# Layer 0's front in another order, values made there, and the maxima's transfers on one queue

## The chip, the core and the metric

One core of a Trainium2 chip runs the whole program in one launch. The metric is the device time of an execution in microseconds; lower is better. TensorE, VectorE (DVE), ScalarE (ACT), GpSimd (POOL) and SyncE (SP) each work through a queue of their own in order, and tell each other by semaphores.

## What is computed

Two layers on x of 32 batches of 256 tokens with 128 channels. Layer 0 is a latent attention with 16 heads, then a top-1 mixture of 8 experts; layer 1 is a windowed attention with pooled latents, then a top-8 mixture of 64 experts. What the change touches is layer 0:

```
xn     = layernorm(x)
latent = xn @ latent_w + latent_b            # 36 columns: keys and values
q      = xn @ Wd_w[h] + Wd_b[h]              # per head
attn   = softmax(causal(q @ latent.T / sqrt(8)))
y      = attn @ latent
x      = x + concat_heads(y) @ out_w + out_b
logits = xn @ Wr + br                        # 8 experts, from the same normalised tokens
```

## The kernel before

Tokens stand in 64 tiles of 128, in eight chunks of eight tiles (XCH, XT). Two heads form a pair (eight pairs), two pairs a group (four groups).

The **front** makes, chunk by chunk: statistics on VectorE (stats0, lines 930 to 938), mean and deviation on GpSimd (deviation0, 617 to 627), normalised rows on ScalarE (norm, 1482 to 1486), transposes on TensorE into two PSUM banks (chunk, 1781 to 1788), their evacuation by ScalarE (chunk, 1488 to 1490) and VectorE (turned, 940 to 942), and the routing logits of the chunk, eight columns for each tile (logits, 1790 to 1798). Beside them run, for the first batch, keys and values (kv, 1800 to 1808), queries (qproj, 1810 to 1820, evacuated by qevac, 1492 to 1497), their casts to bf16 on GpSimd (round_keys and round_queries, 642 to 651), and the row maxima: a score product of a pair (smax, 1822 to 1834), reduced on VectorE (red, 954 to 963) and turned (turn_maxima, 965 to 970). The order of each engine's work in the front is written out by hand (TensorE 1949 to 1984, ScalarE 1530 to 1553, VectorE 1102 to 1132, GpSimd 687 to 704).

The transfers of x are all issued by SyncE: the first chunk at once (331), the other three pieces behind the small weights (342 to 344).

The **steps** follow, one for each batch b, while the maxima of the next batch n are made; a loop holds steps 2 to 29. TensorE's order in a step (1896 to 1947) mixes scores of n (smax), queries of n, the output projection of b-2 (outp), scores of b (st_first, st_second), and the product with the values (av_first, av_second) of four groups. All groups of av share one bank, bankB, which ScalarE evacuates after each (yevac, 1513 to 1515); av_first of the next group waits for that. Between the third and the fourth group stands kv of the batch after the next:

```
                av_first(b, 2, True)
                av_second(b, 2)
                if m:
                    kv(m)
                av_first(b, 3, True)
                av_second(b, 3)
```

VectorE evacuates keys and values in its own kv (944 to 952); for the values it waits until the step before has done its products.

The row maxima enter the scores as two extra rows of the queries: four transfers of 4 KB from mT into qT, two issued by SyncE as soon as mT is there (maxima, 354 to 358), two by ScalarE at the end of its step, behind the last evacuation (maxima, 1499 to 1503, called at 1528). st_first of a batch waits for all four (1839). SyncE's queue then holds, in each step, the denominators of the batch (360 to 388). In the 16 steps of batches 2 to 17 GpSimd also scatters the normalised rows to the sorted order of the experts (scatter_rows, 637 to 640), between round_keys and round_queries.

## Time and profile before

| | us |
|---|---|
| runs, median of 3 (lowest to highest) | 1732.88 (1728.96 to 1735.12) |
| the profiled execution | 1733.61 |
| its span | 1731.9 |
| busy TensorE, VectorE, ScalarE, GpSimd | 1502.6, 1156.0, 992.2, 922.6 |

The profile is of one execution; its time lies 0.7 us above the median. The span is cut into stretches by what TensorE does: the front up to about 97 us, the steps of layer 0's attention to about 796, then the experts of layer 0, layer 1 and its experts, which the change does not touch. In the profile's rows a matmul of fp32 data is two records, one for each of its two passes; PE is TensorE's matmuls, PEld its weight loads; a row "x8" merges eight neighbours of one kind, and what stands in brackets is the idle time of the engine before it and who ended it. SPq and ACTq are transfers issued by SyncE and ScalarE.

### The profile page before, as it was taken

The page shows a single profiled execution, that of the slowest core. Times are in us where ns is not written, and L with a number is a line of the kernel's source. Part 1 is how long each engine was busy: PE and PEld are TensorE (multiplying, and loading weights), DVE is VectorE, ACT ScalarE, POOL GpSimd, SP SyncE. Part 2 cuts the span into 40 slices and gives each one's busy share as a digit, 9 for nine tenths or more (in the row PEclk, how much of TensorE's full clock was granted, in tenths as well). Part 3 has the DMA queues.
Part 4 walks back from the last instruction along what each step waited for, and adds up shares of the span by engine and source line. Part 5 has one row for each costly group of instructions (what it writes and reads, how often), then busy time and mean ns, then how long its engine had stood idle before and what let it go on. Part 6 is the DMA issues. An engine that isn't in the chain of part 4 may idle for free.

```text
span 1731.9 us, 44291 instructions
## 1 busy us (share of the span) xinstructions
PE 1502.6 (87%) x12962; PEld 1083.1 (63%) x12963; DVE 1156.0 (67%) x4123; ACT 992.2 (57%) x2494; POOL 922.6 (53%) x1627
## 2 busy tenths in 40 slices
PE   4789999999999999998996788888888888875883
PEld 4644555555555555556996577777777777764772
DVE  3356656666666666654553599988999989876661
ACT  3334555555555555553331788887888888852431
POOL 4235566666654444434444566666666666623663
PEclk9998999999999999999998699999999999996665
DMA  7103222222222222234332122112112121116444
GB/s 199 36 7 79 63 62 62 62 62 62 62 56 56 62 62 62 69 77 99 68 71 48 28 45 43 44 43 46 42 41 44 44 46 42 42 28 130 88 84 117
DMA packets 240984, 107.60 MB, mean 62 GB/s; under 512 B 145561, under 2 KB 229338, under 8 KB 240858
## 3 DMA queue, kind: packets, MB, share of 16 engines
q1 hardware_dynamic: 228506, 92.97, 22.4%
q0 software_dynamic: 10240, 13.64, 3.7%
q8 instruction: 26, 0.43, 0.1%
q10 hardware_dynamic: 2176, 0.26, 0.1%
q14 instruction: 36, 0.29, 0.1%
HBM read 61.92 MB, written 40.16 MB: 59 GB/s over the span
## 4 chain that ended last, share of the span: by engine, by line
PE 59%; ACT 17%; issue 6%; POOL 6%; DVE 5%; DMA 5%; SPq 1%; POOLq 0%; ACTq 0%; DVEq 0%
PE bankT L1843 8%; PE bankB L1866 8%; PE bankA L1818 7%; PE bankT L2018 4%; PE bankB L1873 3%; PE bankT L1852 3%; ACT pe L1592 3%; DMA qT<-mT 3%; ACT qx L1606 3%; ACT km L1615 2%; PE bankB L1882 2%; ACT gqx L1606 2%; PE bankB L2081 2%; PE bankS L2007 2%; PE bankT L2007 2%
## 5 line engine op out<-in xcount | busy, mean ns | idle before, releaser
L958 DVE CUSTOM_DVE_ANT_0 masked<-bankS,causal 128x128 bf16<-128x128 f32 x512 | 128.6, 289 | 224.0 <-PE bankS L1833 220.0
L658 POOL TENSOR_SCALAR_AFFINE_SELECT probs<-probs 128x512 f32<-128x512 f32 x256 | 171.4, 693 | 146.3 <-ACT probs L1507 146.0
L1507 ACT ACTIVATE probs<-bankT 128x1024 f32<-128x1024 f32 x128 | 131.2, 1025 | 123.5 <-PE bankT L1843 123.5
L961 DVE CUSTOM_DVE_ANT_0 masked<-bankS,causal 128x256 bf16<-128x256 f32 x512 | 195.7, 420 | 0.1
L651 POOL CAST qb<-qT 128x256 bf16<-128x256 f32 x256 | 100.3, 414 | 170.1 <-ACT qT L1496 169.9
L1496 ACT ACTIVATE qT<-bankA,bd 128x256 f32<-128x256 f32 x256 | 107.3, 470 | 117.7 <-PE bankA L1818 113.6
L1818 PE MATMUL bankA<-xnT,wd 128*128 128x256 f32 x512 | 153.5, 425 | 0.0
L1843 PE MATMUL bankT<-qT,kT 37*128 37x512 f32 x512 | 147.1, 651 | 6.5 <-DMA qT<-mT 5.8
L1866 PE MATMUL bankB<-probs,vaug 128*64 128x512 f32 x512 | 139.9, 625 | 1.6 <-ACT yT L1515 1.4
L1309 DVE STREAM_TRANSPOSE pt<-pe 128x768 f32<-128x768 f32 x128 | 124.4, 972 | 24.2 <-ACT pe L1592 24.2
L1515 ACT COPY yT<-bankB 128x512 f32<-128x512 f32 x128 | 74.9, 585 | 113.0 <-PE bankB L1873 113.0
L2137 PE MATMUL bankT<-vx,pt 128*64 128x68 f32 x1024 | 72.4, 228 | 54.1 <-ACT gkm L1635 54.1
L1818 PEld LDWEIGHTS bankA<-xnT,wd 128*128 128x128 f32 x512 | 91.6, 199 | 34.2 <-issue 26.3
L1592 ACT ACTIVATE pe<-pr 128x768 f32<-128x768 f32 x128 | 108.0, 844 | 7.3 <-DVE pr L1303 5.0
L2137 PEld LDWEIGHTS bankT<-vx,pt 128*64 128x64 f32 x1024 | 55.6, 137 | 66.8 <-ACT gkm L1635 34.7
L724 POOL COPY probs<-shelf 128x516 f32 x72 | 44.8, 623 | 77.3 <-DVE qT L1195 74.4
L762 POOL DMA_INDIRECT yg<-ys_sorted,idx_g x64 | 65.9, 1029 | 36.8 <-POOL gate_g L758 26.4
L1873 PEld LDWEIGHTS bankB<-probs,vaug 128*64 128x64 f32 x512 | 37.2, 138 | 74.4 <-issue 73.5
L2018 PE MATMUL bankT<-shelf,qT 128*128 x576 | 78.8, 280 | 0.1
L1831 PEld LDWEIGHTS bankS<-kb,qb 36*128 36x128 bf16 x512 | 26.2, 94 | 83.5 <-issue 66.6
L1852 PE MATMUL bankT<-qT,kT 37*128 37x256 f32 x512 | 78.2, 382 | 0.0
L1873 PE MATMUL bankB<-probs,vaug 128*64 128x256 f32 x512 | 77.9, 383 | 0.0
(306 smaller groups left out, 4231.5 us busy)
## 6 DMA issues: line engine op xcount, KB each, us to landing
rzb<-reciprocals SPq DMA_DIRECT2D x128, 128.0 KB
yT<-yT SPq DMA_DIRECT2D x64, 128.0 KB
xtab<-tab SPq DMA_DIRECT2D x32, 192.0 KB, 2.0
xs_sorted<-zeros SPq DMA_DIRECT2D x1, 4608.0 KB, 18.5
qT<-xs_sorted SPq DMA_DIRECT2D x144, 32.0 KB, 1.7
ys_sorted<-qT SPq DMA_DIRECT2D x36, 128.0 KB, 1.9
value_rows<-vrow SPq DMA_DIRECT2D x32, 128.0 KB, 1.8
vx<-value_rows SPq DMA_DIRECT2D x256, 16.0 KB, 1.8
```

The costliest lines, as they stand in the source:

```text
L658: pool.affine_select(out=blocks, in_=blocks, compare_op=ALU.is_ge, fill=0.0, base=0, pattern=[[0, 4], [1, P]], channel_multiplier=-1).then ...
L958: dve.tensor_tensor_reduce(masked[:, e, 0:P], bankS[:, e, 0:P], causal[:, P:2 * P], -1.0, -NEG, ALU.add, ALU.min, mneg[:, n.half, e, j, 0:1])
L961: ins = dve.tensor_tensor_reduce(masked[:, e, P:3 * P], bankS[:, e, P:3 * P], causal[:, :], -1.0, -NEG, ALU.add, ALU.min, mneg[:, n.half, ...
L1507: act.activation(pT[:, g % 2].rearrange("p e j t -> p e (j t)"), bankT[:, 0:2, :], ACT.Exp, scale=SCALE0).then_inc(S["exp_done"], 1)
L1592: act.activation(pe1[:, g % 2].rearrange("p k s q -> p s k q"), pr[:, g % 2, :].rearrange("p (s k q) -> p s k q", k=2, q=W), ACT.Exp, scal ...
L1818: ins = pe.matmul(bankA[:, k * T:(k + 1) * T], wd[:, 2 * r + k, :, :].rearrange("p e l -> p (e l)"), xnT[:, n.half, :], start=True, stop=True)
L1843: ins = pe.matmul(bankT[:, e, :], kT[KEYS[e], u, 0:P], qT[KEYS[e], u, 2 * g:2 * g + 2, :].rearrange("p j t -> p (j t)"), start=True, stop= ...
L1852: ins = pe.matmul(bankT[:, 2 + e, 0:T], kT[KEYS[e], u, P:T], qT[KEYS[e], u, 2 * g:2 * g + 2, P:T], start=True, stop=True, skip_group_check ...
L1866: pe.matmul(bankB[HALVES[e], :], vaug[:, u, 0, :], pT[:, g % 2, e].rearrange("p j t -> p (j t)"), start=True, stop=False, skip_group_check ...
L1873: ins = pe.matmul(bankB[HALVES[e], :].rearrange("p (j t) -> p j t", t=T)[:, :, P:T], vaug[:, u, 1, :], pT1[:, g % 2, e], start=False, stop ...
L2018: ins = pe.matmul(bankY[u][:, 0:C], hT[:, u, k, :], wall[:, bass.ds(e, 1), F0 + KF + k * C:F0 + KF + (k + 1) * C].rearrange("p a c -> p (a ...
L2137: pe.matmul(slots_ps[DL * k:DL * (k + 1), n, 0:PW], pt[:, g, 1, k, 2 * (n % 2):2 * (n % 2) + 2, :].rearrange("p g q -> p (g q)"), vx[:, u, ...
```

## The change

- The order of the front. Four chunks of statistics and deviations run ahead of the first transposes; ScalarE normalises chunk c+1 before it evacuates chunk c, and evacuates queries behind that; transposes have two sets of two banks (rows_ps), so a chunk waits for the evacuation of the chunk before the last. The last three pieces of x are issued by ScalarE, at its begin. GpSimd's constant blocks of layer 1 move behind the deviations.
- One product in the front (latents) makes values and logits of all tokens, 44 columns for each tile, into lv_all; VectorE adds the biases. The value products and their evacuation leave the steps; GpSimd copies the values of a batch from lv_all (values), behind the wait that VectorE had.
- All four transfers of the maxima are issued by SyncE.
- To make room in SBUF two tables of the routing lie in the place of the experts' second bias, which is loaded behind the loop instead of in the front.

The diff, cut to its core (renumbered waits on the routing's semaphore, lists of names, the old addition of the logits' bias and the orders by hand of three engines are left out, the orders standing below it; eight columns of indent are dropped):

```diff
@@ -80,6 +80,7 @@
+rows_ps = [[bankT[:, 0, :], bankT[:, 1, :]], [bankT[:, 2, :], bankB[:, :]]]
@@ -117,7 +118,8 @@
-lg_all = sb("lg_all", [P, NT, E0])
+lv_all = sb("lv_all", [P, NT, LR])
+lg_all = lv_all[:, :, L:LR]
@@ -140,9 +142,9 @@
-eq0 = sb("eq0", [P, NT, E0])
+eq0 = b2all[:, 0:E0 // 2, :].rearrange("p e (n k) -> p (e n) k", k=E0)
...
-tot0 = sb("tot0", [P, NT, E0])
+tot0 = b2all[:, E0 // 2:E0, :].rearrange("p e (n k) -> p (e n) k", k=E0)
@@ -339,9 +341,6 @@
-    for k in range(1, len(SPANS)):
-        rows = slice(SPANS[k][0] * XT, SPANS[k][1] * XT)
-        sp.dma_start(xa_all[:, rows, :], xv[:, rows, :]).then_inc(S[f"x_in{k}"], 16)
@@ -349,11 +348,10 @@
-    sp.dma_start(b2all[:, :, :], a["L0_ffn_b2"].rearrange("(o e) c -> o e c", o=1).to_broadcast([P, E0, C])).then_inc(S["w_in"], 16)
...
-        for k in range(P // W // 2):
+        for k in range(P // W):
@@ -415,7 +413,9 @@
-        elif k < E0 + KF:
+        elif k == E0 + KF:
+            sp.dma_start(b2all[:, :, :], a["L0_ffn_b2"].rearrange("(o e) c -> o e c", o=1).to_broadcast([P, E0, C])).then_inc(S["w_ex"], 16)
+        else:
@@ -435,7 +435,7 @@
-    for k in range(2 * (LOOP - CLEARED), E0 + KF):
+    for k in range(2 * (LOOP - CLEARED), E0 + KF + 1):
@@ -634,6 +634,12 @@
+    def values(n):
+        if not (type(n.pair) is int and n.pair == 0):
+            pool.wait_ge(S["av_done"], (n.b - 1) * GROUPS)
+            passed(pool)
+        pool.tensor_copy(vaug[:, n.half, :, 0:L], lv_all[:, bass.ds(n.b * 2, 2), 0:L]).then_inc(S["va_sb"], 1)
@@ -661,6 +667,7 @@
+            values(n)
@@ -939,17 +947,17 @@
-        dve.tensor_copy(xnT_all[:, c * XT * P + 512:c * XT * P + 1024], bankT[:, 1, :]).then_inc(S["xt_dve"], 1)
+        dve.tensor_copy(xnT_all[:, c * XT * P + 512:c * XT * P + 1024], rows_ps[c % 2][1]).then_inc(S["xt_dve"], 1)
+    def latents(c):
+        dve.wait_ge(S["lv_ps"], c + 1)
+        dve.tensor_tensor(lv_all[:, c * XT:(c + 1) * XT, :], bankT[:, 3, 0:XT * LR].rearrange("p (k l) -> p k l", k=XT),
+                          lbr[:, :].unsqueeze(1).to_broadcast([P, XT, LR]), ALU.add).then_inc(S["lv_sb"], 1)
...
-        if not (type(n.pair) is int and n.pair == 0):
-            dve.wait_ge(S["av_done"], (n.b - 1) * GROUPS)
-        values = keys_ps[:, 0, T:T + 2 * L].rearrange("p (t l) -> p t l", t=2)
-        dve.tensor_tensor(vaug[:, u, :, 0:L], values, lbr[:, 0:L].unsqueeze(1).to_broadcast([P, 2, L]),
-                          ALU.add).then_inc(S["va_sb"], 1)
@@ -1487,7 +1495,7 @@
-        act.copy(xnT_all[:, c * XT * P:c * XT * P + 512], bankT[:, 0, :]).then_inc(S["xt_act"], 1)
+        act.copy(xnT_all[:, c * XT * P:c * XT * P + 512], rows_ps[c % 2][0]).then_inc(S["xt_act"], 1)
@@ -1495,12 +1503,6 @@
-    def maxima(n):
-        act.wait_ge(S["mT_sb"], n.b + 1)
-        for k in range(P // W // 2, P // W):
-            act.dma_start(qT[L:LP + L + 1:LP, n.half].rearrange("e j (t k q) -> e (j t) k q", t=2, q=W)[:, :, k],
-                          mT[W * k:W * (k + 1), n.half, :]).then_inc(S[f"m_in{n.half}"], 16)
@@ -1524,32 +1526,20 @@
             if g:
                 yevac(b, g - 1)
         yevac(b, GROUPS - 1)
-        if n:
-            maxima(n)

     first, second = Batch(0, 0), Batch(0, 1)
+    for k in range(1, len(SPANS)):
+        part = slice(SPANS[k][0] * XT, SPANS[k][1] * XT)
+        act.dma_start(xa_all[:, part, :], xv[:, part, :]).then_inc(S[f"x_in{k}"], 16)
     norm(0)
-    chunk(0)
-    norm(1)
-    chunk(1)
-    norm(2)
-    chunk(2)
-    act.wait_ge(S["w_a"], 16 * NA)
-    qevac(first, 0)
-    norm(3)
-    chunk(3)
-    qevac(first, 1)
-    norm(4)
-    chunk(4)
-    qevac(first, 2)
-    norm(5)
-    chunk(5)
-    qevac(first, 3)
-    norm(6)
-    chunk(6)
-    norm(7)
-    chunk(7)
-    maxima(first)
+    for c in range(XCH):
+        if c + 1 < XCH:
+            norm(c + 1)
+        chunk(c)
+        if c == 2:
+            act.wait_ge(S["w_a"], 16 * NA)
+        if 2 <= c < 2 + GROUPS:
+            qevac(first, c - 2)
     qevac(second, 0)
     step(first, second, Batch(1, 0))
     act.wait_ge(S["te_go"], 1)
@@ -1780,32 +1770,30 @@
-        if c:
-            pe.wait_ge(S["xt_act"], c)
-            pe.wait_ge(S["xt_dve"], c)
+        if c >= 2:
+            pe.wait_ge(S["xt_act"], c - 1)
+            pe.wait_ge(S["xt_dve"], c - 1)
...
-            ins = pe.transpose(bankT[:, k // 4, (k % 4) * P:(k % 4 + 1) * P], xn_all[:, c * XT + k, :], ident[:, :])
+            ins = pe.transpose(rows_ps[c % 2][k // 4][:, (k % 4) * P:(k % 4 + 1) * P], xn_all[:, c * XT + k, :], ident[:, :])
...
-    def logits(c):
+    def latents(c):
...
+        if c:
+            pe.wait_ge(S["lv_sb"], c)
...
-            ins = pe.matmul(bankT[:, 3, t * E0:(t + 1) * E0], xnT_all[:, t * P:(t + 1) * P], lwr[:, L:LR], start=True, stop=True,
+            ins = pe.matmul(bankT[:, 3, k * LR:(k + 1) * LR], xnT_all[:, t * P:(t + 1) * P], lwr[:, :], start=True, stop=True,
...
-        if c == XCH - 1:
-            ins.then_inc(S["rk_ps"], 1)
+        ins.then_inc(S["lv_ps"], 1)
...
-        u = n.half
...
-        if keys_ps is bankT:
+        if not (type(n.pair) is int and n.pair == 0):
...
-        pe.matmul(keys_ps[:, 0, 0:T], lw[:, :, :].rearrange("p e l -> p (e l)"), xnT[:, u, :], start=True, stop=True)
-        for t in range(2):
-            ins = pe.matmul(keys_ps[:, 0, T + t * L:T + (t + 1) * L], xnT[:, u, t * P:(t + 1) * P], lwr[:, 0:L], start=True, stop=True)
-        ins.then_inc(S["kv_ps"], 1)
+        pe.matmul(keys_ps[:, 0, 0:T], lw[:, :, :].rearrange("p e l -> p (e l)"), xnT[:, n.half, :],
+                  start=True, stop=True).then_inc(S["kv_ps"], 1)
@@ -1823,8 +1811,6 @@
-            if type(n.pair) is int and n.pair == 0:
-                pe.wait_ge(S["va_sb"], n.b + 1)
@@ -1855,8 +1841,10 @@
+        if g == 0:
+            pe.wait_ge(S["va_sb"], b.b + 1)
...
-            pe.wait_ge(S["rk_sb"], 3)
+            pe.wait_ge(S["rk_sb"], 2)
@@ -1909,7 +1897,7 @@
-            pe.wait_ge(S["va_sb"], n.b + 1)
+            pe.wait_ge(S["kv_sb"], n.b + 1)
```

The orders of the front on the other engines, from the diff (red, smax and qproj with a number are those of the first batch):

```
GpSimd before:  deviation0(0) layer1_blocks deviation0(1) fetch(first) fetch(second) deviation0(2) round_keys(first)
                deviation0(3) round_queries(first, 0) deviation0(4) round_queries(first, 1) deviation0(5)
                round_queries(first, 2) deviation0(6) round_queries(first, 3) deviation0(7) round_queries(second, 0)
GpSimd after:   deviation0(0 to 3) fetch(first) fetch(second) deviation0(4) round_keys(first) deviation0(5)
                round_queries(first, 0) deviation0(6) round_queries(first, 1) deviation0(7) values(first)
                round_queries(first, 2) layer1_blocks round_queries(first, 3) round_queries(second, 0)
VectorE before: stats0(0) stats0(1) turned(0) stats0(2) turned(1) kv(first) stats0(3) turned(2) stats0(4) turned(3)
                red 0  stats0(5) turned(4) red 1  red 2  stats0(6) turned(5) red 3  red 4  stats0(7) turned(6) red 5
                turned(7) red 6  red 7  turn_maxima(first) best kv(second)
VectorE after:  stats0(0 to 3) turned(0) stats0(4) turned(1) stats0(5) latents(0) kv(first) turned(2) stats0(6)
                latents(1) turned(3) stats0(7) latents(2) turned(4) latents(3) red 0  turned(5) red 1  latents(4)
                red 2  turned(6) red 3  latents(5) red 4  turned(7) red 5  latents(6) red 6  latents(7) red 7
                turn_maxima(first) kv(second)
TensorE before: chunk(0) chunk(1) logits(0) kv(first) chunk(2) logits(1) qproj 0  chunk(3) logits(2) smax 0  qproj 1
                chunk(4) logits(3) smax 1  qproj 2  smax 2  chunk(5) logits(4) smax 3  qproj 3  smax 4  chunk(6)
                logits(5) smax 5  chunk(7) logits(6) smax 6  logits(7) smax 7  kv(second) qproj(second, 0) step(first)
TensorE after:  chunk(0) chunk(1) latents(0) kv(first) qproj 0  chunk(2) latents(1) chunk(3) latents(2) qproj 1
                chunk(4) latents(3) smax 0  qproj 2  chunk(5) smax 1  latents(4) smax 2  qproj 3  chunk(6) smax 3
                latents(5) smax 4  chunk(7) smax 5  latents(6) smax 6  latents(7) smax 7  kv(second) qproj(second, 0)
                step(first)
```

## Rows read from the trace of the kernel before

**Rows 1.** Busy us by stretch: PE, PEld, DVE, ACT, POOL, granted clock, DMA share, GB/s

```profile
13.00:97.00 84.00, 58.45 (x256) 50.52 (x256) 32.76 (x192) 30.58 (x74) 21.81 (x42) 1.00 0.36 102
24.00:34.00 10.00, 10.00 (x45) 9.73 (x46) 5.66 (x35) 3.78 (x10) 2.63 (x5) 1.00 0.37 95
500.00:755.00 255.00, 255.00 (x1664) 138.99 (x1664) 161.27 (x865) 140.88 (x240) 110.23 (x217) 1.00 0.25 63
```

**Rows 2.** Timeline of one chunk of the front: start, us, engine, line, what [idle before]

```profile
51.01 1.97 PE L1787 MATMUL bankT<-ident,shelf 128*128 128x128 f32 x8 [3.99 <-ACT shelf L1485]
...
52.77 3.42 PE L1795 MATMUL bankT<-lwr,xnT_all 128*128 128x8 f32 x16
...
56.56 2.08 PE L1818 MATMUL bankA<-xnT,wd 128*128 128x256 f32 x4
...
58.67 0.84 ACT L1496 ACTIVATE qT<-bankA,bd 128x256 f32<-128x256 f32 x2 [5.07 <-PE bankA L1818]
...
59.40 3.17 ACT L1485 ACTIVATE shelf<-xa_all,xshift,xrstd 128x128 f32<-128x128 f32 x8
...
62.63 1.97 PE L1787 MATMUL bankT<-ident,shelf 128*128 128x128 f32 x8 [3.56 <-ACT shelf L1485]
```

**Rows 3.** Timeline, begin and end of the front

```profile
13.10 1.94 PE L1787 MATMUL bankT<-ident,shelf 128*128 128x128 f32 x8 [13.10 <-ACT shelf L1485]
...
97.19 0.29 PE L1831 MATMUL bankS<-kb,qb 36*128 36x128 bf16 x2 [2.04 <-POOL kb L645]
```

**Rows 4.** Query products of line 1818 alone: busy (count), granted clock, DMA

```profile
33.00:60.00 27.00, 6.20 (x12) 1.00 0.62 180
116.00:118.00 2.00, 1.13 (x4) 1.00 0.03 8
137.50:140.00 2.50, 2.07 (x4) 0.53 0.33 53
```

**Rows 5.** Timeline, value products of the front

```profile
27.55 0.91 PE L1807 MATMUL bankS<-lwr,xnT 128*128 128x36 f32 x4
```

**Rows 6.** Transfers of x: landing times (tile view), and three issues (timeline)

```profile
DMA to landing us min/median/max: 3.7/6.3/15.0
...
8.89 5.62 SPq L344 DMA_DIRECT2D xa_all<-in_L_attn_x  x3
```

**Rows 7.** Timeline of TensorE, end of a loop step and of a last step

```profile
646.49 0.60 PE L1873 MATMUL bankB<-probs,vaug 128*64 128x256 f32 x4
...
647.55 0.53 PE L1807 MATMUL bankT<-lwr,xnT 128*128 128x36 f32 x4
648.01 1.08 PE L1866 MATMUL bankB<-probs,vaug 128*64 128x512 f32 x4
...
773.02 0.60 PE L1873 MATMUL bankB<-probs,vaug 128*64 128x256 f32 x4
774.31 1.08 PE L1866 MATMUL bankB<-probs,vaug 128*64 128x512 f32 x4 [0.69 <-ACT yT L1515]
```

**Rows 8.** Maxima in the loop: waits (200 to 490), timeline, chain

```profile
PE bankT L1843 <- DMA qT<-mT: 5.8, 12, 0.9
...
369.04 1.16 SPq L357 DMA_DIRECT2D qT<-mT  x2
...
375.94 1.13 PE L1843 MATMUL bankT<-qT,kT 37*128 37x512 f32 x4 [0.43 <-DMA qT<-mT]
...
371.53 0.52 ACT yT L1515
...
372.09 3.73 DMA qT<-mT
```

**Rows 9.** Timeline of GpSimd in the same step

```profile
371.42 0.99 POOL L639 DMA_INDIRECT xs_sorted<-shelf,pos_all  x1 [0.29 <-issue]
...
374.41 0.41 POOL L635 COPY xnT<-xnT_all 128x256 f32<-128x256 f32 x1
...
378.31 1.22 POOL L658 TENSOR_SCALAR_AFFINE_SELECT probs<-probs 128x512 f32<-128x512 f32 x2 [1.10 <-ACT probs L1507]
```

More of the change, by code:

```diff
@@ L687, in _ @@
             first, second = Batch(0, 0), Batch(0, 1)
-            deviation0(0)
-            layer1_blocks()
-            deviation0(1)
+            for c in range(4):
+                deviation0(c)
             fetch(first)
             fetch(second)
-            deviation0(2)
+            deviation0(4)
             round_keys(first)
-            deviation0(3)
+            deviation0(5)
             round_queries(first, 0)
-            deviation0(4)
+            deviation0(6)
             round_queries(first, 1)
-            deviation0(5)
+            deviation0(7)
+            pool.wait_ge(S["lv_sb"], 1)
+            passed(pool)
+            values(first)
             round_queries(first, 2)
-            deviation0(6)
+            layer1_blocks()
             round_queries(first, 3)
-            deviation0(7)
             round_queries(second, 0)
@@ L1102, in _ @@
             first, second = Batch(0, 0), Batch(0, 1)
[L1103 to L1105 removed]
+            for c in range(4):
+                stats0(c)
             dve.wait_ge(S["w_a"], 16 * NA)
             dve.wait_ge(S["consts"], 1)
[L1108 removed]
+            turned(0)
+            stats0(4)
             turned(1)
+            stats0(5)
+            latents(0)
             kv(first, bankS)
[L1111 removed]
             turned(2)
[L1113 removed]
+            stats0(6)
+            latents(1)
             turned(3)
+            stats0(7)
+            latents(2)
+            turned(4)
+            latents(3)
             red(first, 0)
[L1116 to L1117 removed]
+            turned(5)
             red(first, 1)
+            latents(4)
             red(first, 2)
[L1120 to L1121 removed]
+            turned(6)
             red(first, 3)
+            latents(5)
             red(first, 4)
[L1124 to L1125 removed]
+            turned(7)
             red(first, 5)
[L1127 removed]
+            latents(6)
             red(first, 6)
+            latents(7)
             red(first, 7)
             turn_maxima(first, False)
[L1131 to L1132 removed]
+            kv(second)
+            dve.wait_ge(S["lv_sb"], XCH)
             onehot(0)
@@ L1953, in _ @@
             pe.wait_ge(S["w_a"], 16 * NA)
-            logits(0)
+            latents(0)
+            pe.wait_ge(S["xt_act"], 1)
             kv(first, bankS)
+            qproj(first, 0)
             chunk(2)
-            logits(1)
-            qproj(first, 0)
+            latents(1)
             chunk(3)
-            logits(2)
-            smax(first, 0)
+            latents(2)
             qproj(first, 1)
             chunk(4)
-            logits(3)
+            latents(3)
+            smax(first, 0)
+            qproj(first, 2)
+            chunk(5)
             smax(first, 1)
-            qproj(first, 2)
+            latents(4)
             smax(first, 2)
-            chunk(5)
-            logits(4)
+            qproj(first, 3)
+            chunk(6)
             smax(first, 3)
-            qproj(first, 3)
+            latents(5)
             smax(first, 4)
-            chunk(6)
-            logits(5)
+            chunk(7)
             smax(first, 5)
-            chunk(7)
-            logits(6)
+            latents(6)
             smax(first, 6)
-            logits(7)
+            latents(7)
             smax(first, 7)
-            pe.wait_ge(S["red_done"], PAIRS)
-            kv(second, bankS)
+            pe.wait_ge(S["xt_act"], XCH)
+            pe.wait_ge(S["xt_dve"], XCH)
+            kv(second)
             qproj(second, 0)
-            pe.wait_ge(S["rk_sb"], 1)
+            pe.wait_ge(S["lv_sb"], XCH)
             step(first, second, None, Batch(1, 0), False)
```

36 lines of the change are left out of this document (8 added, 28 removed).

## The prediction

> **What bounds the kernel now.** I read the busy time by stretch first, then the order of time inside the front, then the waits of TensorE, then the chain of waits around each edit. In the loop of layer 0 TensorE is busy in 255.00 of 255 us, so only what shortens TensorE's own queue, or fills a gap in it, counts there [rows 1]. In the front (13 to 97 us) it is busy in 58.45 of 84 us, and VectorE, ScalarE and GpSimd in less than 33 each: no engine is full, and what sets the time is who waits for whom [rows 1].
>
> One turn of the front shows the loop of waits. From the transposes of one chunk (51.01) to those of the next (62.63) pass 11.6 us. TensorE transposes, multiplies the logits of the chunk before, takes one product of row maxima, and projects queries (56.56). Only then can ScalarE evacuate the queries (58.67), and its normalisation of the next chunk stands behind that evacuation in its queue (59.40, 3.17 us); TensorE waits 3.56 us for it [rows 2]. So the pitch is TensorE's work plus ScalarE's, one after the other. After the front the first step begins with the maxima of the second batch at 97.19 us [rows 3].
>
> **The clock of the front.** The granted clock reads 1.00 in the front, but its twelve query matmuls take 6.20 us, 0.52 each, as the four at granted 0.53 do (2.07, 0.52 each), while four at granted 1.00 in the loop take 1.13, 0.28 each [rows 4]. So the front runs at the 1.2 GHz level throughout, and I price it with its own rows.
>
> **The change, part by part.**
>
> Front order. Statistics run four chunks ahead, the transposes have two sets of PSUM banks, and normalisation of chunk c+1 now stands ahead of the evacuation of chunk c and of the queries. ScalarE's part drops out of the pitch, and the front should become TensorE's queue. Its work: the stretch from transposes over one product to one score product is 56.56 - 51.01 = 5.55 us per chunk, eight times 44.4 [rows 2]. Five query projections at 2.05 (2.08 with the tail of the last matmul) are 10.3 [rows 2]. The keys are two matmuls of the same form as four of a projection, so about 1.0, twice: 2.0. Sum 56.7.
>
> Start. The first transposes begin at 13.10 [rows 3]. The first chunk of x landed 3.7 us after its issue, alone [rows 6]; now three more transfers of x leave on ScalarE's queue at the same moment and share the engines, which at worst doubles the 3.7. I take half of that, +1.8. TensorE then waits once for the second normalisation, 3.17 - 1.76 (a chunk's transposes, 51.01 to 52.77) = 1.4 [rows 2]. The tail, queries evacuated and cast before the first step, stays 2.04 [rows 3]. Sum: 13.1 + 1.8 + 1.4 + 56.7 + 2.0 = 75.0, against 97.19: **-22.2 us**. ScalarE is not the limit: 8 x 3.17 + 4 x 0.84 = 28.7 plus eight evacuations. The three issues of x took SyncE 5.62 us from 8.89 [rows 6]; on ScalarE they start near 1 and are over before its first normalisation, near 13.1 + 1.8 - 3.2 = 11.7: cost 0. A late last piece of x would cost: its statistics stand ahead of the second evacuation on VectorE. It landed 15.0 us after its issue [rows 6]; issued some 8 us earlier it is in time, but the zeroing of the sorted rows now follows sooner on SyncE, and if that keeps x as late as before I estimate +4. The constant blocks of layer 1 move on GpSimd from the first chunk to behind the deviations; it is idle for 62 of 84 us there [rows 1]: 0.
>
> One product for values and logits. Eight output columns become 44 in each of 64 products of two matmul records each. Four matmuls of 36 columns took 0.91 us, 0.23 each; 16 of 8 columns took 3.42, 0.21 each [rows 5, 2]. The four carry the same tail as the sixteen, so I take the width at 0; upper bound 0.02 x 128 = 2.6. VectorE's eight wider evacuations replace one, beside the 51 us that it has free [rows 1].
>
> Loop, TensorE. Each of 30 steps (batches 2 to 31) loses the four value matmuls, 647.55 to 648.01, or 0.46 us [rows 7]. But the next product writes the bank that ScalarE is still evacuating. Where no keys stand in between (last steps) the same place, second to third group, takes 774.31 - 773.02 = 1.29, ended by that evacuation; with keys and values it takes 648.01 - 646.49 = 1.52 [rows 7]. So only 0.23 of the 0.46 come through, and the evacuation is late next: 30 x 0.23 = **-6.9 us** (bounds 0 and 30 x 0.46 = 13.8).
>
> Maxima all on SyncE. In the first half of the loop TensorE waited 12 times for the maxima's transfer, 5.8 us in all [rows 8]. The last one is ScalarE's: it is issued behind the last evacuation of the step (371.53) and lands 3.73 us after 372.09. SyncE had its pair out from 369.04, 0.58 each. With four there, the last starts at 369.04 + 3 x 0.58 = 370.78 and lands at 374.51. TensorE wants it at 375.94 - 0.43 (its wait) - 0.23 (the gain above) = 375.28 [rows 8]. So the wait goes, with 0.8 us to spare: **-5.8 us**. The two more issues on SyncE end at 371.36, before it has to take the denominators of the step, which wait for that evacuation (371.53 + 0.52); ScalarE's two were off the path.
>
> Values on GpSimd. A copy of 128x72 per step, no dearer than the 0.41 of 128x256, behind a wait for the last product of the step before. Queued behind it are the scatter of rows, the cast of the next queries and the clip. The wait ends about when the first scatter began anyway (371.42; the last evacuation, released by the same product, starts at 371.53), so all of it is pushed by at most 0.5; before the clip GpSimd was idle for 1.10 [rows 9]. TensorE comes 0.66 earlier, so this cover is just used up: cost 0, and up to 0.5 in each of 16 scattering steps, 8 us, if it is not. VectorE loses an addition and a wait in each step; it waits for the score product next anyway.
>
> Rest. The bias rows of the experts now load behind the loop, 512 KB as the first chunk of x, which took 3.7 [rows 6]; TensorE's last batch hides it. Cost 0, up to 3.7 without that cover. The old logits pass and the additions after the front lay on VectorE beside TensorE: 0.
>
> **Sum.** -22.2 - 6.9 - 5.8 = -34.9 against the profiled execution's 1733.6 us (span 1731.9): 1698.7. That execution lies 0.7 above the median of the runs, 1732.9, so I predict **1698 us**.
>
> **Rivals.**
>
> A. TensorE goes to the 2.4 GHz level in the front. For: it would now be dense for 57 us. Against: it was busy 10.00 of 10 us at 24 to 34 [rows 1] and the query products behind that still took 0.52 [rows 4]. By it the queue needs half, and ScalarE becomes the bound: 28.7 plus about 5 for evacuations from 11.7 (its first normalisation), then some 9 for the last scores, keys and queries: 54, so -43; the first step, at the low level now, gains some 7: with the loop 1733 - 43 - 7 - 12.7 = 1670. In between (the level rises for some stretches) lie 1685 to 1695. The Trainium skill (TensorE: Matmul & The Clock Gate, Part 1) has the low clock as the default that sustained activity releases; by that rule alone this case would be the forecast, and the dense stretch just named, which released nothing, speaks against it.
>
> B. The change does not do what it says: queues keep the front at its old pitch, because in-order score products wait for casts that stand behind deviations on GpSimd. For: each order is still fixed by hand. Against: deviations need only statistics, which are done early. The front then gives 0 to 10: 1710 to 1720.
>
> C. The loop gives nothing: GpSimd's wait eats what TensorE gains. 1733 - 22 = 1711. Against: the 1.10 of idle time [rows 9].
>
> D. Slower: four transfers on one queue are served one after another. Against: ScalarE's two, issued half a microsecond apart, were both there at 375.82 [rows 8]. Each microsecond beyond 375.28 costs 30 us over 30 steps; from 1.2 us beyond it all is lost. Served singly the last lands at 369.04 + 4 x 3.73 = 383.96, 8.7 late: 1698 + 260 = 1958.
>
> **How the numbers follow.** Forecast 0.66, A 0.13, B 0.08, C 0.09, D 0.04. The forecast's bounds (x late +4, 2.6, 8, 3.7, hardly all at once; or the full 0.46, -7, and a few low-clock stretches less) give 1685 to 1712. The range adds C and half of A and B: 1676 to 1714; about 0.17 is left out. A measurement of this kernel tells 0.3%, about 5 us, from no change. All but D and the edge of B lie below 1727: faster 0.92, same 0.03, slower 0.05.
>
> **What would show it.** Right: a chunk pitch near 7.6 us with TensorE idle under 1 us in it, the first step near 75, query products at 0.52 in the front, no wait of TensorE for the maxima, and the third group's product ended by the evacuation, 1.29 behind the second. Wrong: waits for casts or normalisation inside the front; query products of 0.28 there; a wait for the maxima of over a microsecond per step.

## The result, and the profile after

The kernel after takes 1687.26 us (median of 4 runs, 1682.85 to 1689.08), the kernel before beside it 1730.92 (4 runs, 1727.41 to 1735.12): 43.7 us less, ratio 0.9742, 95% interval 0.9718 to 0.9766. Forecast were 1698 us, in a range of 1676 to 1714. The profiled execution took 1689.08 us.

The page of the kernel after, its span and its busy times:

```profile
span 1687.3 us, 44051 instructions
...
PE 1470.3 (87%) x12833; PEld 1046.1 (62%) x12835; DVE 1149.8 (68%) x4098; ACT 993.0 (59%) x2496; POOL 931.1 (55%) x1659
```

To see where the 44.6 us between the two spans come from, I set the same instruction of both traces side by side at several places (keys are the product of kv, once per step):

| place | before | after | lead of after |
|---|---|---|---|
| first step (maxima of the second batch) [rows 3] | 97.19 | 63.41 | 33.8 |
| keys of batch 3 | 147.32 | 114.22 | 33.1 |
| keys of batch 6 | 217.22 | 179.66 | 37.6 |
| keys of batch 19 (end of the scattering steps) | 498.92 | 452.07 | 46.9 |
| keys of batch 31 | 752.80 | 703.49 | 49.3 |
| first product of the experts | 796.52 | 748.91 | 47.6 |
| third product of the experts | 799.59 | 753.22 | 46.4 |
| end | 1731.9 | 1687.3 | 44.6 |

So the front gave 33.8 us where 22.2 were forecast; the loop 16.2, where 12.7 were; the start of the experts took back 3, where nothing was expected. The last 1.8 arise in the last part of the program, which the change does not touch: behind the last product with wo1 (the output weights of layer 1's attention) before takes 175.1 us, after 176.9, and a second profile of the kernel after (the run "again") 171.2.

**The front.** Its timeline, with TensorE's rows, the long issues of SyncE and VectorE's first evacuation:

```profile
7.06 3.39 SPq L337 DMA_DIRECT2D bd<-in_L_attn_Wd_b  x1
...
12.40 2.57 SPq L342 DMA_DIRECT2D lwr<-in_L_ffn_Wr  x1
...
15.01 0.64 SPq L343 DMA_DIRECT2D lbr<-in_L_ffn_br  x1
...
23.42 0.69 DVE L950 COPY xnT_all<-bankT 128x512 f32<-128x512 f32 x1 [8.30 <-DMA lbr<-in_L_ffn_br]
...
24.25 3.61 PE L1787 MATMUL bankT<-lwr,xnT_all 128*128 128x44 f32 x16 [5.02 <-DVE xnT_all L950]
...
28.65 1.91 PE L1806 MATMUL bankA<-xnT,wd 128*128 128x256 f32 x4
...
37.47 1.11 PE L1806 MATMUL bankA<-xnT,wd 128*128 128x256 f32 x4
...
51.19 0.66 PE L1777 MATMUL bankT<-ident,shelf 128*128 128x128 f32 x4 [0.68 <-ACT shelf L1493]
...
59.56 1.91 PE L1806 MATMUL bankA<-xnT,wd 128*128 128x256 f32 x4
...
63.41 0.29 PE L1817 MATMUL bankS<-kb,qb 36*128 36x128 bf16 x2 [1.93 <-POOL kb L651]
```

The chain's piece for the last small weight (start, us, what):

```profile
15.01 8.38 DMA lbr<-in_L_ffn_br
```

Three things are to be seen. The gaps of 3.56 us and more before a chunk [rows 2] are gone: after 24.25 no wait of TensorE is longer than 0.9 us until the tail of 1.93, and none for a normalisation longer than 0.68. The price of the four query matmuls is 1.91 at 28.65, 1.11 at 37.47 and 1.91 again at 59.56, against 2.08 in the same place before [rows 2]: for most of the chunks TensorE runs at the 2.4 GHz level. And there is a new wait of 5.02 us near the begin: VectorE's first evacuation stands behind a wait for the small weights, which land only at 23.4, because x now comes in beside them (x_third, below, moves 2 MB of x away). The stretches by level:

```profile
14.28:32.27 17.99, 11.92 (x50) 10.51 (x50) 7.31 (x46) 10.10 (x27) 9.46 (x17) 1.00 0.91 216
32.27:56.17 23.90, 21.81 (x183) 18.93 (x182) 19.06 (x100) 18.39 (x46) 11.62 (x30) 0.99 0.38 107
56.17:63.41 7.24, 5.31 (x21) 3.87 (x21) 2.58 (x13) 0.84 (x2) 1.26 (x4) 0.50 0.02 4
```

(Columns as in [rows 1].) The second stretch is the one of short products. As in the kernel before, the granted clock reads 1.00 ahead of the first rise too; only the durations tell the level there.

**The loop.** Third and fourth group of a late step:

```profile
577.25 0.60 PE L1861 MATMUL bankB<-probs,vaug 128*64 128x256 f32 x4
577.78 0.70 PE L1795 MATMUL bankT<-xnT,lw 128*128 128x256 f32 x2
578.53 1.08 PE L1854 MATMUL bankB<-probs,vaug 128*64 128x512 f32 x4
```

From av_second to the next av_first pass 1.28 us (forecast 1.29, before 1.52 [rows 7]). The twelve late steps (batches 19 to 31) take 20.95 each instead of 21.16: 0.21 less. The 13 scattering steps from batch 6 to 19 take 20.95 instead of 21.67, 0.72 less, and TensorE has no wait for the maxima [rows 8] left. The three steps from batch 3 to 6 take 65.4 us instead of 69.9, 4.5 less, where 0.21 each would be 0.6. Rows of the last of them: VectorE's evacuation of the values and TensorE's wait in the kernel before, then the same wait in the kernel after:

```profile
196.99 0.23 DVE L951 TENSOR_TENSOR vaug<-bankT,lbr 128x72 f32<-128x72 f32 x1 [0.96 <-PE bankB L1873]
...
200.95 0.23 PE L1831 MATMUL bankS<-kb,qb 36*128 36x128 bf16 x2 [1.56 <-DVE mneg L961]
```

```profile
163.38 0.23 PE L1817 MATMUL bankS<-kb,qb 36*128 36x128 bf16 x2 [0.23 <-DVE mneg L969]
```

Before, VectorE waited 0.96 us for the products of the step before it could take the values; the rest of the routing's tables stood behind that, and behind the tables the reductions of the row maxima, for which TensorE's next score product waits. With the values on GpSimd the tables follow the keys at once, and 1.56 us of waiting become 0.23. In the two steps ahead of it TensorE's waits for GpSimd's casts are shorter (2.25 instead of 2.44, none instead of 0.57), and a stretch of 3.4 us at the 1.2 GHz level behind the first of them (granted 0.50 from 153.5) is gone; which part of the change did that was not tried by itself. So the loop's 16.2 us are 28 x 0.205 = 5.7 in TensorE's queue, 6.6 more in the scattering steps from batch 6 on and 3.9 more in these three.

**The start of the experts.** The timeline of SyncE's last issue, GpSimd's first copy of weights and TensorE, and the chain's piece for that transfer:

```profile
739.97 1.12 SPq L417 DMA_DIRECT2D b2all<-in_L_ffn_b  x1
...
747.81 0.61 POOL L732 COPY probs<-shelf 128x516 f32 x1 [5.82 <-issue]
...
748.91 2.05 PE L1997 MATMUL bankS<-probs 128*128 128x128 f32 x8 [2.51 <-POOL probs L733]
750.75 1.73 PE L1997 MATMUL bankT<-probs 128*128 128x128 f32 x8
...
753.22 1.06 PE L1997 MATMUL bankS<-probs 128*128 128x128 f32 x8
```

```profile
739.97 6.46 DMA b2all<-in_L_ffn_b
```

The second bias is issued last of the experts' weights, behind the reciprocals of the last steps, and lands 6.46 us later; GpSimd's copies wait for it, and TensorE waits 2.51 us for them, where it waited 0.92 before. Behind that gap two groups of products run at the 1.2 GHz level, 2.05 and 1.73 us instead of 1.13 and 1.06, and the lead shrinks by another 1.2 us.

### The profile page after: what moved, and what is told of

Its sections match the earlier page's. It is cut to its first block, busy times and chain, and to the rows that moved or that the text cites. A ratio compares the mean times of both kernels' runs of the same rounds, so it can differ in the third digit from the quotient of the medians.

```text
span 1687.3 us, 44051 instructions
## 1 busy us (share of the span) xinstructions
PE 1470.3 (87%) x12833; PEld 1046.1 (62%) x12835; DVE 1149.8 (68%) x4098; ACT 993.0 (59%) x2496; POOL 931.1 (55%) x1659
## 4 chain that ended last, share of the span: by engine, by line
PE 63%; ACT 16%; issue 5%; DVE 5%; POOL 4%; DMA 4%; SPq 1%; POOLq 0%; another core or an unknown queue 0%; ACTq 0%; DVEq 0%
PE bankA L1806 8%; PE bankT L1829 8%; PE bankB L1854 7%; PE bankT L2008 4%; PE bankB L1870 3%; PE bankT L1838 3%; PE bankB L1861 3%; ACT qx L1596 3%; ACT km L1605 2%; ACT gqx L1596 2%; PE bankT L2127 2%; PE bankA L2109 2%; ACT rows L1669 2%; PE bankT L2132 2%; PE bankT L1997 2%
## 5 line engine op out<-in xcount | busy, mean ns | idle before, releaser
L1806 PE MATMUL bankA<-xnT,wd 128*128 128x256 f32 x512 | 149.4, 415 | 0.0
L1806 PEld LDWEIGHTS bankA<-xnT,wd 128*128 128x128 f32 x512 | 89.9, 195 | 33.4 <-issue 25.7
L926 POOL DMA_INDIRECT acc<-ym,aidx x32 | 52.0, 1624 | 45.7 <-ACT ym L1755 17.5
```

The lines of the kernel that those rows point to most:

```text
L1806: ins = pe.matmul(bankA[:, k * T:(k + 1) * T], wd[:, 2 * r + k, :, :].rearrange("p e l -> p (e l)"), xnT[:, n.half, :], start=True, stop=True)
```

## The experiments

Runs of one group shared a chip and the runs of the kernel before; three groups ran on three chips. A ratio is to the kernel before of the same group, with its 95% interval. The kernel after itself has ratio 0.9742 above and 0.9697 in the third group (the run "again", 1682.68 us), 4.6 us apart in time; so differences of some us between groups tell nothing, and where a gain is that small the traces are read, not the medians.

**One part alone: the maxima on SyncE** (maxima_sp, against the kernel before)

```diff
-                for k in range(P // W // 2):
+                for k in range(P // W):
...
-                if n:
-                    maxima(n)
```

> The kernel before, with one part of the change alone: all four transfers of the maxima issued by SyncE. My theory: the 12 waits of TensorE for these transfers in the first half of the loop go, 5.8 us; about 1725 us, ratio 0.9966, steps of that half shorter by about 0.45 us on average, the later steps unchanged. Rival 1: ScalarE's pair only hid another lateness and the wait stays or moves: 1731. Rival 2: four transfers on one queue are served one after another: slower by tens of us.

1725.08 us against 1731.8, ratio 0.9957 (0.9934 to 0.9979): 6.7 us less. The keys of two scattering steps in a row:

```profile
319.21 0.70 PE L1796 MATMUL bankT<-xnT,lw 128*128 128x256 f32 x2
340.37 0.70 PE L1796 MATMUL bankT<-xnT,lw 128*128 128x256 f32 x2
```

21.16 us, what the late steps take; before, 12 of the 13 scattering steps from batch 6 to 19 were longer, 21.5 to 22.1, and the 13 took 6.6 us more than here. The three steps from batch 3 to 6 take 69.8, as before. Alone, this part does what was forecast.

**The same part undone in the kernel after** (split: two transfers on ScalarE again; the diff is the reverse)

> The kernel after, with two of the four transfers of the maxima issued by ScalarE again, at the end of its step. Theory: the waits of TensorE for them come back; the loop is 0.2 us shorter per step now, so they are somewhat longer than the 5.8 us of the kernel before: 6 to 9 us more than the kernel after, first half of the loop 21.3 to 21.5 per step instead of 20.97. Rival: in the kernel after something else in the step has become the limit, and less than 3 us come back.

The rival holds. The 13 scattering steps take 272.4 us as in after, no wait for the maxima comes back, and the keys of batch 31 stand at 703.65 (703.49 in the first profile of after). The medians, 1688.11 beside 1682.68 for the kernel after in the same group (ratios 0.9723, 0.9693 to 0.9753, and 0.9697, 0.9668 to 0.9727), would have been read as 5.4 us coming back; the profiles of split and again differ by 7.2, and 1.5 of that is there before the loop, none arises in it, the rest comes behind it. Why the part is worth nothing here is in the order of two queues. ScalarE's transfers and GpSimd's work in a scattering step of this run, and below ScalarE's issue in the kernel before:

```profile
328.81 1.07 ACTq L1510 DMA_DIRECT2D qT<-mT  x2
328.94 0.24 POOL L641 COPY vaug<-lv_all 128x72 f32<-128x72 f32 x1 [0.66 <-PE bankB L1870]
...
329.62 0.99 POOL L645 DMA_INDIRECT xs_sorted<-shelf,pos_all  x1 [0.44 <-issue]
```

```profile
371.54 1.07 ACTq L1502 DMA_DIRECT2D qT<-mT  x2
```

Before, the first scatter started at 371.42 [rows 9], 0.12 us ahead of the transfers; now GpSimd's new copy of the values stands ahead of the scatters and waits for the last product of the step, so they start 0.81 us behind the transfers. The packets of ScalarE's two transfers, in the traces, tell what goes with that: in the kernel before, the last one ends 3.5 to 4.1 us behind the first issue in the 12 steps that wait, 3.15 in the one scattering step among them that does not (issued at 328.76), and 2.8 to 2.9 in the late steps, which have no scatters and no wait; in split it ends after 2.7 to 3.0 us in every step from 200 us on. One step of before, issued at 414.74, narrows it: there the scatter starts 0.20 us behind the first of the two issues, but ahead of the second, and TensorE waits 0.55 all the same. So two parts of the change each take the same wait away, and it can be taken once. (That it is the scatters' traffic that delays the transfers goes with all of these steps, but was not tried by itself.)

**The value products put back** (vals, against the kernel after)

```diff
+                if not (type(n.pair) is int and n.pair == 0):
+                    for t in range(2):
+                        ins = pe.matmul(keys_ps[:, 0, T + t * L:T + (t + 1) * L], xnT[:, n.half, t * P:(t + 1) * P], lwr[:, 0:L],
+                                        start=True, stop=True)
```

> The kernel after, with the four value products of each step put back between the keys and the fourth group's product; they write columns of the bank that nobody reads, so their work is done for nothing. My theory: only half of their 0.46 us comes through, because the next product waits for ScalarE's evacuation anyway: 30 x 0.21 to 0.23 = 6.2 to 6.9 us, 1694, with 1.52 between third and fourth group instead of 1.29. Rival: the full 0.46, 13.8 us, 1701. Rival 2: nothing.

1689.09 us (ratio 0.975, 0.972 to 0.9779), less than the 1694 expected; the medians cannot tell it from the kernel after. The loop shows it better:

```profile
583.38 0.60 PE L1866 MATMUL bankB<-probs,vaug 128*64 128x256 f32 x4
583.91 0.70 PE L1795 MATMUL bankT<-xnT,lw 128*128 128x256 f32 x2
584.44 0.53 PE L1799 MATMUL bankT<-lwr,xnT 128*128 128x36 f32 x4
584.90 0.65 PE L1859 MATMUL bankB<-probs,vaug 128*64 128x512 f32 x2
```

1.52 is back, late steps take 21.16, and from the keys of batch 3 to those of batch 31 pass 594.8 us instead of 589.3: 5.6 in 28 steps, 0.20 each. Of 0.46 us of products less than half comes through. The steps from batch 3 to 6 take 65.9 here, so their further gain of 3.9 does not come from the products: VectorE's evacuation of the values was not put back.

**ScalarE's order undone** (act_order, against the kernel after)

```diff
-                if c + 1 < XCH:
-                    norm(c + 1)
                 chunk(c)
...
                     qevac(first, c - 2)
+                if c + 1 < XCH:
+                    norm(c + 1)
```

> The kernel after, with ScalarE's order of before put back in the front: the normalisation of the next chunk stands behind the evacuation of the chunk and of the queries; all else as after. Theory: this order is what lets TensorE run without gaps, and with it at the 2.4 GHz level: with it undone TensorE waits 2 to 4 us for each normalisation again, query products take 0.52 us in most chunks, the first step begins near 85 to 97 instead of 63.4, time 1708 to 1720. Rival: statistics ahead and two sets of banks are what gave the gain; the first step begins by 70, time 1687 to 1694.

1713.04 us, ratio 0.9895 (0.9866 to 0.9923). Two chunks of its front, and its first step:

```profile
46.96 1.97 PE L1777 MATMUL bankT<-ident,shelf 128*128 128x128 f32 x8 [4.00 <-ACT shelf L1493]
...
52.57 2.08 PE L1806 MATMUL bankA<-xnT,wd 128*128 128x256 f32 x4
58.64 1.12 PE L1777 MATMUL bankT<-ident,shelf 128*128 128x128 f32 x4 [4.00 <-ACT shelf L1493]
...
92.91 0.29 PE L1817 MATMUL bankS<-kb,qb 36*128 36x128 bf16 x2 [1.93 <-POOL kb L651]
```

The pitch of before (11.7 us), its gap and its level are back, with everything else of the change in place. Of the front's 33.8 us, 29.5 hang on two lines of ScalarE's order; the other parts of the front bring 4.3 without it.

**Is it the width or the gaps that set TensorE's level?** Three runs. The kernel before with logit products of 44 columns (bwide; the columns of lwr change places to fit, not shown):

```diff
-                    ins = pe.matmul(bankT[:, 3, t * E0:(t + 1) * E0], xnT_all[:, t * P:(t + 1) * P], lwr[:, L:LR],
+                    n = min(LR, NT * E0 - t * E0)
+                    ins = pe.matmul(bankT[:, 3, t * E0:t * E0 + n], xnT_all[:, t * P:(t + 1) * P], lwr[:, 0:n],
```

> The kernel before, with nothing changed but the width of the front's logit products: 44 columns instead of 8 (the extra columns are overwritten by the next products; result and order are as before). Theory 'width': it is the wider products that took TensorE to the 2.4 GHz level in the front of the kernel after; then query products of the front take 0.28 us each instead of 0.52 in most chunks, TensorE's 5.5 us per chunk falls by up to half, and the first step begins some 10 to 20 us before 97.2: 1711 to 1721 us. Theory 'order': it is the gaps between the chunks that held the level down; then the front stays at 0.52, the first step stays near 97 to 99 and the time near 1731 to 1733.

1731.94 against 1731.8 (ratio 1.0002, 0.9975 to 1.0029); first step at 97.42, queries at 2.07. Width alone does nothing in a front with gaps. The kernel after with products of 8 columns (narrow; VectorE's addition is narrowed to match and the values are set to zero, not shown):

```diff
-bankT[:, 3, k * LR:(k + 1) * LR], xnT_all[:, t * P:(t + 1) * P], lwr[:, :],
+bankT[:, 3, k * LR + L:(k + 1) * LR], xnT_all[:, t * P:(t + 1) * P], lwr[:, L:LR],
```

> The kernel after, with the front's products 8 columns wide instead of 44: only the logits; the values of layer 0 are left at zero, so that the attention of layer 0 has no values, with as many instructions and waits. Theory 'width': the front stays at the 1.2 GHz level, query products take 0.52 there, the first step begins near 75 to 82 instead of 63.4, and the time is 1698 to 1706. Theory 'order': the level rises near 32 us as in the kernel after, first step near 62 to 63, time near 1687.

1693.71 us (ratio 0.9776, 0.9747 to 0.9805), first step at 69.45: neither number. Its four query products take 1.91, 1.20, 2.08 and 1.13 in turn; the level rises in two pieces of 6.8 us, and for a short third one just ahead of the first step. Kernels with 44 columns show pieces too (below), so this run leaves open whether width helps to hold the level. The kernel before with its gaps filled by work for nothing (filled):

```diff
             def chunk(c):
+                if c >= 2:
+                    for k in range(16):
+                        pe.transpose(bankT[:, 2, (k % 4) * P:(k % 4 + 1) * P], ident[:, :], ident[:, :])
                 pe.wait_ge(S["xn_done"], c + 1)
```

> The kernel before, with 16 transposes of the identity put into TensorE's queue ahead of its wait for each normalisation of chunks 2 to 7 (their results go to a free bank and are not read): work for nothing, about 3.6 us of it at the 1.2 GHz level, in place of a wait of 3.56 us. Theory: the gaps between the chunks are what keeps TensorE at 1.2 GHz in the front; filled, the level rises near 30 us and stays, query products take 0.28 us, and the front gets shorter although TensorE does more: first step near 80 to 88 instead of 97.2, 1714 to 1722. Rival: not the gaps, and the front stays at 0.52 with the first step at 97 to 100: 1731 to 1735.

TensorE's timeline in its front:

```profile
28.13 3.48 PE L1784 MATMUL bankT<-ident 128*128 128x128 f32 x16
...
34.02 1.11 PE L1821 MATMUL bankA<-xnT,wd 128*128 128x256 f32 x4
...
60.70 1.13 PE L1821 MATMUL bankA<-xnT,wd 128*128 128x256 f32 x4
...
86.61 0.29 PE L1834 MATMUL bankS<-kb,qb 36*128 36x128 bf16 x2 [2.04 <-POOL kb L645]
```

1723.18 us against 1734.0, ratio 0.9939 (0.9914 to 0.9963): 96 useless transposes make the kernel 10.8 us faster, a little less than expected. Its queries take 1.11 in one chunk, 2.08 and 2.03 in the next two, 1.13 in the last; the first step comes 10.6 us earlier. By the granted clock TensorE has 30.7 us at the 2.4 GHz level ahead of the first step, in four pieces; the four kernels with waits of 2.8 to 4.5 us before their chunks have none (before, bwide) or 3.4 (maxima_sp, act_order), the nine with after's order on ScalarE 15.3 (narrow) to 25.4. So the gaps keep the level down in the front of the kernel before. They are not all that decides it: in after the level falls at 55.85, where no wait since 35.69 was longer than 0.68 us, and why it does stays open. The Trainium skill (TensorE: Matmul & The Clock Gate, Part 1) has the low clock as the default that activity releases; the run with the filled gaps agrees, useless activity does.

**The small weights** (x_third, against the kernel after: the last 2 MB of x on SyncE behind them)

```diff
+            sp.dma_start(xa_all[:, SPANS[3][0] * XT:SPANS[3][1] * XT, :], xv[:, SPANS[3][0] * XT:SPANS[3][1] * XT, :]).then_inc(S["x_in3"], 16)
...
-            for k in range(1, len(SPANS)):
+            for k in range(1, len(SPANS) - 1):
```

> The kernel after, with the last and largest piece of x (2 MB) issued by SyncE behind the small weights instead of by ScalarE at its begin. Theory: the small weights are late because x is in their way (the last of them issued at 15.0 and landed at 23.4); without the 2 MB they land before 19, the first product of values and logits starts right behind the second chunk's transposes, near 19.3 instead of 24.25, and the front ends up to 5 us earlier: 1682 to 1684. Rival 1: the front is bound by something else from there on (ScalarE's pitch of 4.3 us, the later piece of x) and the time stays at 1687. Rival 2: the last piece of x is now late for the fifth chunk's statistics (at 24.0 in the kernel after) and the front gets longer, by some us.

Timeline of its front, TensorE and VectorE:

```profile
19.07 3.48 PE L1788 MATMUL bankT<-lwr,xnT_all 128*128 128x44 f32 x16
...
24.22 1.64 DVE L942 BATCH_NORM_STATS2 xstat<-xa_all 128x6 f32<-128x128 f32 x8 [7.13 <-DMA xa_all<-in_L_attn_x]
...
29.90 3.61 PE L1788 MATMUL bankT<-lwr,xnT_all 128*128 128x44 f32 x16 [3.62 <-DVE lv_all L955]
```

1688.83 us, ratio 0.9736 (0.9703 to 0.977): nothing gained. The first product starts at 19.07 as said, but VectorE now waits 7.13 us for x ahead of the evacuation that TensorE needs, and TensorE loses 3.62 there: rival 2. So its order was mended (x_stats):

```diff
             turned(0)
-            stats0(4)
             turned(1)
-            stats0(5)
             latents(0)
             kv(first, bankS)
+            stats0(4)
             turned(2)
-            stats0(6)
+            stats0(5)
             latents(1)
```

(stats0(6) and stats0(7) likewise one place later)

> The kernel after, with the last piece of x (2 MB) on SyncE behind the small weights, as in the run before, and VectorE's order mended for it: the statistics of chunks 4 to 7 stand behind the first evacuation of values and logits, so that their wait for x holds up nothing. Theory: both waits go (5.0 us of TensorE for the small weights in the kernel after, 3.6 us for VectorE behind x in the run with the piece moved alone); the second product of values and logits starts near 26 instead of 32.0 and the front ends 4 to 6 us earlier: 1681 to 1683. Rival: what the front gains the clock takes: TensorE stays longer at 1.2 GHz, time 1686 to 1689.

1681.12 us, ratio 0.9706 (0.9679 to 0.9734): the time that was expected, but the kernel after measured again, 1682.68 (0.9697), would fit as well, so the time does not show the gain. The trace does. The second product of values and logits starts at 25.96 instead of 32.02; the first step only at 60.75, 2.7 earlier, since the level rises in three short pieces (queries 1.47, 1.13 and 1.51 us). The keys of batch 3 come at 107.69, in the two profiles of the kernel after at 114.22 and 112.85.

**The second bias inside the loop** (b2_early, against the kernel after)

```diff
                 experts(2 * (i - CLEARED) + 1)
+                if i == CLEARED:
+                    experts(E0 + KF)
-            for k in range(2 * (LOOP - CLEARED), E0 + KF + 1):
+            for k in range(2 * (LOOP - CLEARED), E0 + KF):
```

> The kernel after, with the experts' second bias loaded inside the loop (in its tenth turn, once the routing tables in its place are done) instead of behind the loop. Theory: the load stood last in SyncE's queue behind the reciprocals of the last step, held GpSimd's first copy of weights and with it TensorE for 2.5 us, and the gap was followed by 3.4 us at the 1.2 GHz level; with it early the start of the experts is as in the kernel before (a wait of about 0.9 us), some 3 us earlier: 1684. Rival: the experts' start is bound by the sorted rows that are loaded there too, and the time stays at 1687.

TensorE's first products of the experts, in the timeline:

```profile
747.23 1.13 PE L1999 MATMUL bankS<-probs 128*128 128x128 f32 x8 [0.92 <-DVE probs L1212]
748.20 1.06 PE L1999 MATMUL bankT<-probs 128*128 128x128 f32 x8
```

1681.33 us, ratio 0.971 (0.9684 to 0.9737); here too only the trace shows a gain. The wait is that of before, 0.92, and no slow products follow. In eight profiles with the bias behind the loop TensorE waited between 1.08 and 3.19 us here.

**Both mends** (best), beside **the kernel after once more** (again), in one group

> The kernel after with both mends: the second bias of the experts loaded inside the loop, the last piece of x behind the small weights with VectorE's statistics of chunks 4 to 7 behind the first evacuation of values and logits. Theory: the two gains lie in different places (front, start of the experts) and add up: 2 to 3 us and 3 to 6 us below the kernel after measured beside it, some 1679. Rival: the clock's levels in the front and behind move as much as that, and it lies within 3 us of either mend alone: 1681.

> The kernel after, unchanged (a blank line more), as the measure for the others of this group: 1687, and the part of the program behind the attention of layer 0 within some us of 983.8 us, the same level of the clock in its front as in its first profile if that level is set by the work, another one if it is not.

The first step in the timeline of again, and of best:

```profile
62.63 0.23 PE L1818 MATMUL bankS<-kb,qb 36*128 36x128 bf16 x2 [1.93 <-POOL kb L651]
```

```profile
59.01 0.23 PE L1820 MATMUL bankS<-kb,qb 36*128 36x128 bf16 x2 [1.94 <-POOL kb L654]
```

Best takes 1679.12 us (ratio 0.9683, 0.9652 to 0.9715), again 1682.68 (0.9697, 0.9668 to 0.9727). The 3.6 us between the medians are less than these intervals can tell apart. In the profiles best is ahead by 3.6 us at the first step (the rows above) and by 6.9 at the keys of batch 31 (695.29 against 702.15), but only by 1.2 at the end (1676.2 against 1677.4): stages that both share were slower in that execution. The two profiles of the kernel after show how much those stages move: from the keys of batch 31 to the end 983.8 us in the first, 975.3 in again.

## Why the prediction was right, and where it was not

The time lies in the range, 11 us below the forecast, at the place that rival A gave to a front that is fast for some stretches (1685 to 1695). That it is no further off is in part luck: in the profiles the front gave 11.6 us more than forecast and the loop 3.5, while 5.4 were lost behind the first step, at the start of the experts and at the end, where nothing was forecast. By its steps:

- **Front, right in its cause.** "ScalarE's part drops out of the pitch": with ScalarE's order undone 29.5 of the 33.8 us go away again.
- **Front, wrong in its price: "So the front runs at the 1.2 GHz level throughout, and I price it with its own rows."** This is the step that failed. The argument against rival A, that the dense stretch at 24 to 34 us had released nothing, was one stretch of one execution: with the same front in maxima_sp the level did rise there, at 30.08. What the prediction took for the level of this work was the level of a front with gaps, as the filled gaps show. In after, 21.8 us of products ran at the high level, in 23.9 us. At the low one, by my estimate, they would take 1.84 times as long (2.08 against 1.13 for four query matmuls), 40.1: 16.2 us more than the stretch took. With the 11.9 and 5.3 us of the other two stretches that is 57.3 us of work, where the prediction had 56.7: the work was right, its level was not.
- **Start: "cost 0" for the issues of x.** I asked when x would be late, not what x would make late. The small weights cost TensorE 5.0 us. The three terms close the sum: -22.2 + 5.0 - 16.2 = -33.4, measured -33.8.
- **Loop, TensorE: right.** 0.23 of 0.46 forecast, 0.21 measured, and 0.20 with the products put back; the evacuation is "late next", 1.28 against 1.29.
- **Maxima on SyncE: right, but not the only part that does it.** Forecast -5.8; alone 6.7 by the medians, and 6.6 by the trace in the 13 steps from batch 6 to 19, a little more than the waits I had counted. In the finished kernel, undone, it gives nothing back, because the values' wait on GpSimd, which I priced at 0 with a bound of +8, holds the scatters behind the transfers and takes the same wait away. I had looked at that wait as a cost only.
- **Values off VectorE, put at nothing: "it waits for the score product next anyway."** In a step that has the routing's tables it does not: they stood behind the values, and TensorE's wait for VectorE's reductions, 1.56 us, fell to 0.23. The three steps from batch 3 to 6 gained 3.9 us beyond the products. The maxima on SyncE alone do not bring it (69.8 us), and with the products put back it stays (65.9). This is what the loop gave beyond the forecast.
- **Bias behind the loop: "TensorE's last batch hides it. Cost 0, up to 3.7."** It does not: the load is issued last of the experts' weights, behind the last reciprocals, and takes 6.46 us. It cost 1.6 us of waiting and 1.2 more at the low level, within the bound.
- **Rivals.** A came true for half of the front. B, that hand-written orders keep the pitch, did not: 4.3 us per chunk from 38.41 to 51.19. C fell with the loop's 0.21 and 0.72, D with maxima_sp.

## What to carry to other kernels

Gaps cost TensorE twice: once as idle time, and once more as slower products around them; before trusting durations from a stretch with gaps, price the closed stretch at both levels, and where one can't tell, fill the gaps with idle work and look. When work leaves an engine, look at what stands behind it in that engine's queue in every kind of step, and not only in the usual one. When two edits remove the same wait, undo each in the finished kernel: a gain that one edit shows alone may be worth nothing in company. When a transfer is moved forward, ask which small ones it now runs beside, and when one is moved behind a loop, what stands ahead of it in the queue.

## What the runs showed of the hardware that was not expected

The level in the front is not the same from one execution to the next. The front of the kernel before stayed low until 110 to 113 us in its own profile and in that of bwide; with the same front in maxima_sp it rose for 3.4 us near 30 us and fell back. In four kernels with after's dense front it was high for 23.9 us in one piece (after, b2_early, split, and best, which has a short second one), in others in shorter pieces, with the same code too: again has 6.8 and 17.1 us with a drop of 3.4 between, where after has one piece. Two short issues on SyncE took 3.39 and 2.57 us while 3.5 MB of x were coming in on ScalarE's queue, where the same two took 0.55 and 0.43 in the kernel before; with 2 MB fewer (x_third) the second was 0.43 again, the first still 3.66. The Trainium skill (DMA: Bandwidth & Descriptors, section "Queues, rings and completion order") says that an engine takes turns between the queues that have work for it; the row agrees in so far as the weights were delayed and not stopped, 8.38 us for 4 KB.
